# Three DMAs and one bias addition moved to other slots of an attention loop on one core

## The reference

```python
def _L0_xattn_ref(x, context, Wq, Wk, Wv, Wo, bo):
    q = x @ Wq.T
    k = context @ Wk.T
    v = context @ Wv.T
    # 16 heads of 32 features
    scores = jnp.einsum('bhqd,bhkd->bhqk', q, k) * SCALE
    scores = jnp.where(causal[None, None, :, :], scores, -jnp.inf)
    probs = jax.nn.softmax(scores, axis=-1)
    y = jnp.einsum('bhqk,bhkd->bhqd', probs, v)
    return y @ Wo.T + bo
...
x = x + jnp.tanh(g_xattn[0]) * _L0_xattn_ref(_layernorm(x, axis=-1), ctx_1024, ...)
x = x + jnp.tanh(g_ffn[0]) * _L0_ffn_ref(_layernorm(x, axis=-1), ...)
```

## Time and profile before

| | us |
|---|---|
| median of three runs | 1888.84 |
| the profiled execution, whole | 1888.26 |
| its span (first to last instruction) | 1886.5 |
| TensorE busy in the span | 1836.9 (97%) |
| VectorE busy | 1475.1 (78%) |
| ScalarE busy | 968.9 (51%) |
| GpSimd busy | 798.4 (42%) |
| TensorE's mean granted clock | 0.993 of full speed |

### The profile page before, as it was taken

The page is one execution under the profiler, slowest core; times in us unless marked ns, Lnnn a source line. Parts: engine busy times, 40 slices in busy tenths (PEclk is TensorE's granted clock), DMA queues, the critical chain, the costliest instruction groups (busy, mean ns, idle before and its releaser), DMA issues.

```text
span 1886.5 us, 32878 instructions
## 1 busy us (share of the span) xinstructions
PE 1836.9 (97%) x11316; PEld 1554.4 (82%) x11316; DVE 1475.1 (78%) x3241; ACT 968.9 (51%) x2260; POOL 798.4 (42%) x1043
## 2 busy tenths in 40 slices
PE   6999999999998999999999999999999999999999
PEld 6899999999997678888778887877888887888887
DVE  6788988888887777777877777797777777877776
ACT  5787888888888533333433343343333434433332
POOL 3445555555445433443534343453343453333330
PEclk9999999999998999999999999999999999999999
DMA  7888898999984422121141211113212112311111
GB/s 227 178 189 195 198 204 190 213 207 192 205 208 99 136 64 69 56 67 56 34 145 54 81 67 56 46 46 133 87 39 88 45 56 77 104 54 57 45 46 45
DMA packets 207429, 205.60 MB, mean 109 GB/s; under 512 B 104224, under 2 KB 159520, under 8 KB 207264
## 3 DMA queue, kind: packets, MB, share of 16 engines
q1 hardware_dynamic: 207264, 203.50, 42.0%
HBM read 111.43 MB, written 18.87 MB: 69 GB/s over the span
## 4 chain that ended last, share of the span: by engine, by line
PE 72%; DVE 11%; issue 5%; SPq 3%; POOL 3%; ACT 2%; DMA 2%; DVEq 0%; POOLq 0%; ACTq 0%
PE gate_up L1310 31%; PE down L1824 18%; PE bank L807 14%; SPq L388 2%; DVE ops_lo L1167 2%; PE scores L910 2%; DVE acc L1675 2%; PE probs_t L944 2%; POOL hidden L1523 1%; DMA turned<-halves 1%; PE rows_t L797 1%; PE y L934 1%; PE y L932 1%; SPq L404 1%; PE down L1803 1%
## 5 line engine op out<-in xcount | busy, mean ns | idle before, releaser
L1310 PE MATMUL gate_up<-xo_hi,ops_hi 128*128 128x512 f32 x1120 | 440.5, 393 | 14.2 <-DVE gated L1286 5.4
L1310 PE MATMUL gate_up<-xo_hi,ops_lo 128*128 128x512 f32 x1120 | 436.6, 390 | 0.0
L1310 PE MATMUL gate_up<-xo_lo,ops_hi 128*128 128x512 f32 x1120 | 436.5, 390 | 0.0
L1310 PEld LDWEIGHTS gate_up<-xo_hi,ops_hi 128*128 128x128 f32 x1120 | 210.5, 188 | 68.0 <-DVE gated L1286 10.6
L1675 DVE SCALAR_TENSOR_TENSOR acc<-down,scale,acc 128x512 f32<-128x512 f32 x320 | 238.2, 745 | 35.0 <-PE down L1824 34.4
L616 ACT ACTIVATE probs<-probs,neg_max 128x128 f32<-128x128 f32 (+1 forms) x512 | 229.2, 449 | 69.4 <-DVE neg_max L739 65.2
L1824 PE MATMUL down<-d_hi,h_hi 128*128 128x512 f32 x640 | 249.1, 389 | 0.0
L1824 PE MATMUL down<-d_hi,h_lo 128*128 128x512 f32 x640 | 249.1, 389 | 0.0
L1824 PE MATMUL down<-d_lo,h_hi 128*128 128x512 f32 x640 | 249.1, 389 | 0.0
L1310 PEld LDWEIGHTS gate_up<-xo_lo,ops_hi 128*128 128x128 f32 x1120 | 210.5, 188 | 44.2
L1310 PEld LDWEIGHTS gate_up<-xo_hi,ops_lo 128*128 128x128 f32 x1120 | 210.6, 188 | 42.4
(11 more groups left out here) (191 smaller groups left out, 4438.9 us busy)
## 6 DMA issues: line engine op xcount, KB each, us to landing
g_raw<-in_w_gate SPq DMA_DIRECT2D x40, 512.0 KB, 3.8
u_raw<-in_w_up SPq DMA_DIRECT2D x40, 512.0 KB, 3.8
d_raw<-in_w_down SPq DMA_DIRECT2D x40, 512.0 KB, 3.7
k_stack<-k_hi SPq DMA_DIRECT2D x128, 128.0 KB, 2.7
q_stack<-q_hi SPq DMA_DIRECT2D x128, 128.0 KB, 2.5
c_in<-in_ctx_t SPq DMA_DIRECT2D x16, 512.0 KB, 4.3
x_in<-in_x SPq DMA_DIRECT2D x16, 512.0 KB, 5.3
k_stack<-k_lo SPq DMA_DIRECT2D x64, 128.0 KB, 2.8
```

Source lines behind the costliest of these rows:

```text
L1310: ins = pe.matmul(gu_ps[bank][:], ops[x][:, which, a, c, :], xo[y][:, b, c, :], start=(begins and c == 0 and i == 0), stop=(c == CH - 1 an ...
```

## The change

Four constants move, and one load is made for another sequence.

- The load of `x_res` goes from slot 2 to slot 4 (`RES_LOAD`), and GpSimd's bias addition from slot 6 to slot 8 (`RES_SLOT`).
- The context's load goes from slot 14, where it was for sequence i + 3, to slot 9 of the next iteration, where it is for i + 2 (`C_LOAD`). ScalarE still reads it in slot 12.
- `store_hat` goes from slot 1 to slot 2.

```diff
-    RES_LOAD, X_LOAD, C_LOAD, ROWS_LOAD = 2, 3, 14, 14
+    RES_LOAD, X_LOAD, C_LOAD, ROWS_LOAD = 4, 3, 9, 14
...
-    RES_SLOT, MOMENTS_SLOT, STD_SLOT, HAT_SLOT = 6, 0, 2, 6
+    RES_SLOT, MOMENTS_SLOT, STD_SLOT, HAT_SLOT = 8, 0, 2, 6
...
-                n, o, ln, far = i + 1, i + -1, i + 2, i + 3
+                n, o, ln = i + 1, i + -1, i + 2
...
-                    if s == 1 and k is not None and k % T == T - 1:
+                    if s == 2 and k is not None and k % T == T - 1:
                         store_hat(k // T)
...
-                    if s == C_LOAD and has(i, 3):
-                        sp.wait_ge(c_lo_made, far.times(1))
-                        sp.dma_start(c_in[:], row(c_v, far)).then_inc(c_loaded, DMA)
+                    if s == C_LOAD and has(i, 2) and has(i, 0):
+                        sp.wait_ge(c_lo_made, ln.times(1))
+                        sp.dma_start(c_in[:], row(c_v, ln)).then_inc(c_loaded, DMA)
```

## The result

The kernel after takes 1911.34 us, the median of 4 runs (1906.68 to 1917.22), beside 1889.1 us for the kernel before on the same chip (4 runs, 1888.53 to 1889.84). The ratio is 1.0118, 95% interval 1.0104 to 1.0131: slower by 22 us. Forecast were 1903 us and a range of 1893 to 1917. The profiled execution took 1910.05 us, of which the span is 1908.3, 21.8 us more than before. The four runs differ in the mean clock that TensorE was granted: 0.994 in those of 1906.68 and 1910.05 us, 0.991 in that of 1912.62 and 0.990 in that of 1917.22. The profiled execution before had 0.993, so its 21.8 us are not the clock.

The account below looks back on a forecast made before the run. The steady iterations were taken as bounded by TensorE's work, busy 458.47 of 460.00 us. The terms 15.2 + 0.6 - 1.0 = 14.8 us on 1888.3 gave 1903 us, range 1893 to 1917.

Parts of the forecast that it names:

- Part a: GpSimd's bias addition, slot 6 to 8: head 8's halves ready 2.7 us later, transpose issued up to 2.1 us later.
- Part c: Context's 512 KB ahead of head 8's transpose: 1.1 us late in iteration 8, no stall from it in iterations 1 and 4.
- Part d: Head 10's transpose moves as head 8's did; iterations lose 1.17 us on average, 15.2 us over thirteen.
- Part b: SyncE's queue: issuing context's load and reload, 0.42 us each, pushes head 8's transpose 0.9 us in iteration 8.
- Part e: Iteration 0, where the context's load is new: head 8's wait grows about 1.8 us, 0.6 us left, bounds 0 and 3.
- Part f: ScalarE's copy of the context waits 0.6 to 2.4 us for the load; taken as 0, up to 1.3 us an iteration.
- Part g: Gains: SyncE's 14.1 us of reload waits go but were hidden; transposes of heads 14, 0, 2 land sooner, 1 us.
- The clock rival: Stalls lower TensorE's clock in five iterations, 17 us more, 1920 us; chance 0.14 for more lost, ScalarE's wait included.

Follow-up runs that it names:

- the stand-ins: Kernels before and after with each transposing DMA replaced by two plain copies of the same blocks; 1893.51 us (ratio 1.0020) and 1936.29 us (1.0238).
- the half-sized load: Against the kernel before with plain copies for transposes: context's load moved to slot 9 with half its bytes (256 KB); 1906.84 us, ratio 1.0081.

## Why the prediction was right, and which terms were off

The direction and the mechanism came out as forecast: transposes of heads 8 and 10 that land late, waited for 13.4 us (forecast about 15). The sum of 14.8 us is 7 short of the profiled 21.8, and the split between the two heads was off: most of the loss is at head 8, where iterations 1 and 4 had it at head 10.

*Part a, the halves late.* Right in place and size: the additions push head 8's halves by 2.7 us. In iteration 8 they begin 2.83 us behind the last Newton step's start in place of 0.15, and the transpose is issued 0.02 us behind their end. The forecast issues can be checked against head 7's product, which waits for neither: counted from it, head 8's transpose is issued 2.1 us later than before in iteration 1, 1.9 in iteration 4 and 0.75 in iteration 8, where +2.1, +1.9 and +0.9 were forecast. Between slots 9 and 8 it is worth 0.49%, about 9 us, in the stand-ins, where nothing else is moved.

*Part c, the landing behind the context's load.* Right in iteration 8 (forecast 4.0 us, measured 4.1). Mis-sized elsewhere: I took 2.8 us where the transpose is issued a microsecond or more behind the load. In iterations 1 and 4 the load is issued at 99.94 and 213.24 and the transpose at 101.45 and 214.29, and it takes 3.8 and 4.3 us to land. The lead of 1.1 to 1.5 us bought nothing, and the upper end that I named, 1.2 us more, was about the value. In iteration 8 the transpose does not stand right behind the load either, but 1.0 us behind its issue. Over iterations 1 to 13 the lead is 0.7 to 2.4 us and the landing 3.3 to 4.6 us. With it the losses at head 8 come out: iteration 1, 2.1 us of issue and 1.0 of landing less 2.3 us of slack is 0.8 (measured 0.9); iteration 4, 1.9 + 1.5 - 2.1 = 1.3 (measured 1.4); iteration 8, 0.75 + 1.3 - 0.9 = 1.1 (measured 1.2). The Trainium skill ("DMA: Bandwidth & Descriptors", section "Queues, rings and completion order"), by which descriptors are taken in order, spoke for that end, and the trace agrees with it; the half-sized load (2.2 to 2.5 us) agrees too.

*Part d, head 10.* In iteration 8 the queue does space the two transposes as before: 5.16 us, before 5.19. In iteration 1 it doesn't. The 6.50 us of before held a stacking copy whose issue took 1.91 us; now the spacing is 5.15 us. The copy, before:

```profile
102.06 1.91 SPq L388 DMA_DIRECT2D q_stack<-q_hi  x1
```

So head 10's transpose moves by 0.7 us there, not by the 2.1 forecast. And head 10's landing is late everywhere: 3.9, 3.6 and 3.8 us in iterations 1, 4 and 8, where I kept 2.8, 2.8 and 3.3. In iteration 1 the two errors cancel, so that 2.1 us forecast against 1.8 measured is luck. The sum per iteration came out differently made in iteration 4 too: I expected 2.1 and 0.3 us at head 10 in iterations 1 and 4 and 1.1 at head 8 in iteration 8; the table above has 1.8, 1.4 and 1.3 us over its rows, half, all and nearly all of it at head 8. As TensorE is late by then, head 10 costs only 0.28 us. This term, 1.17 us forecast and 1.69 measured, is 22.0 in place of 15.2 us, nearly all of what is missing.

*Missing altogether: VectorE.* The forecast moved GpSimd's additions past GpSimd's own queue alone. They run beside VectorE's `y` product, and head 8's halves, which they push, beside its normalisation; the two are lengthened by 0.62 us, and TensorE waits 4.0 us for `t_lo`, of the 16.4 us of added idle time. Alone it is a floor of 0.6 us at heads 7 to 8, as in iterations 3 and 13 of the table; where the transpose is later than that, the two overlap and are not added. The bias addition alone in slot 9 shows the floor with the halves in time. That the instructions are longer is shown; that a shared port is the reason is inferred from where the product ends and from the order in which the normalisation and GpSimd's instruction begin.

*Part b, the queue's issue time.* The reload was charged at 0.42 us of issue and hidden. Its issue is hidden, but its bytes are not: head 4's transpose in iteration 8 takes

```profile
DMA to landing us min/median/max: 5.3/5.3/5.3
```

to land where it was 2.8 (medians over iterations 1 to 13: 5.2 and 3.6), head 6's takes 4.2 in place of 2.8 in the median, and the keys' stacking copies 4.2 in place of 2.7 us. In the real pair the slack of heads 4 and 6, about 3 us each before, swallows that, except at 5 to 6 in iterations 6 and 7 (0.4 and 0.6 us); in the stand-ins the reload costs 0.47%. The forecast had the rule (part c) and used it for the context alone.

*Part e, iteration 0*: 1.8 us up to the stretch in place of 0.6, within its bounds, of which 0.5 us lie ahead of its first product with the values. Head 8's wait grew from 1.2 to 4.1 us and head 10's shrank from 3.5 to 1.8, 1.2 us more together (forecast +1.8 at head 8). *Part f, ScalarE's copy*: 1.7 us in two waits, in iteration 8 the copy starts at 374.25, 0.3 us ahead of head 8's product; no wait of TensorE names it, so 0 was right. *Part g*: the reload's waits are gone and were worth nothing, as said. The 1 us that I had for transposes landing sooner in the steady part did not come. The 2.0 us gained instead lie behind it and go with the clock, so that this term looks right by luck. The clock rival did not come in the profiled execution: one dip in the stretch, 0.57 over 4 us. In two of the other three runs a little of it may have: their mean clock of 0.991 and 0.990 against 0.994 is worth 6 to 8 us of 1910, by the same reckoning, and none was profiled.

Open: why the stand-ins lose 43 us where the real pair loses 22 (the profiled ones 28.5, the rest going in part with their lower clock); what of TensorE's 5.7 us of longer busy time is the clock's dip (some 1.7 us, 4.00 x 0.43, by the third row of the windows) and what the modelled ends; where the rest of the half-sized load's cost lies; and `store_hat`.

## What to carry to other kernels

A load that is moved in a queue is to be charged with its bytes on everything issued in the next microseconds, not with its issue time: here 512 KB delay the landing of the transpose behind them by 1.3 us in the median, with 0.7 to 2.4 us of lead, and that of the next one, 5.2 us later, by 0.8 us. Before an elementwise operation is moved on GpSimd, look at what VectorE does in the place it moves to, and beside what it pushes back, not only at GpSimd's queue. And where the bounding engine has no idle time, count the slack of each waiting instruction in several iterations, with the landing times of the crowded case.

## What the hardware showed that was not expected

- VectorE's normalisation of 128x512 took 0.53 us with nothing beside it, 0.76 to 0.78 us where GpSimd's halves (0.92 us) had begun 0.43 us ahead of it, and 1.13 to 1.15 us where GpSimd's addition of 1.36 us had begun 0.43 us ahead. Where it began ahead of the halves it took 0.53 to 0.54 us. The two-input product of 128x256 took 0.42 us alone and 1.50 us beside the addition.
- A transpose of 128x6x128 in 16 bits landed in 2.8 us (median of head 8 before, iterations 1 to 13), in 3.3 to 4.6 us behind a load of 512 KB issued 0.7 to 2.4 us ahead, and the next one, about 5.2 us later, in 2.9 to 3.9 us.
- The kernel after spreads over 10.5 us in 4 runs, the four runs of the kernel before over 1.3, and the longer ones have the lower granted clock (0.994 at 1906.68 and 1910.05 us, 0.991 at 1912.62, 0.990 at 1917.22). That TensorE's waits lower it in those runs is not shown.
